# Attention scores: two heads side by side in two row halves of TensorE, in three products of 16-bit parts, in place of one head over all rows in two products of 32-bit parts

## The reference

```python
y = x * rsqrt(mean(x * x) + 1e-6) * rms_w
y = einsum('bsm,cm->bsc', y, w_in)                 # q: 32 heads, k: 8, v: 8, each of 64
q, k = rope(q), rope(k)
qk = einsum('bghsd,bgxpd->bghsp', q, k) * 64 ** -0.5
qk = where(causal, qk, -inf)
attn = softmax(qk, axis=-1)
o = einsum('bghsp,bgxpd->bghsd', attn, v)
y = einsum('bsc,mc->bsm', o, w_out)
x = layernorm(x + (x + y))
x = layernorm(x + einsum('bsd,od->bso', ternary(x), ternary(weight) + rram_variation))
```

## Time and profile before

| | |
|---|---|
| Time, median of 3 runs | 1427.19 us (1426.4 to 1428.69) |
| Span of the profiled execution, first to last instruction | 1425.4 us |
| PE busy | 1318.0 us, 92%, 7328 matmuls |
| DVE busy | 1147.2 us, 80% |
| ACT busy | 1116.3 us, 78% |
| POOL busy | 873.7 us, 61% |
| mean granted clock of TensorE | 0.982 of full speed |

### The profile page before, as it was taken

One profiled execution on the slowest core, in us unless ns is written; L12 is line 12 of the kernel. 1 busy time (PEld: TensorE's weight loads), 2 busy tenths in 40 slices (PEclk: granted clock), 3 DMA queues, 4 the chain that ended last, 5 costly groups with the idle time before them and its releaser, 6 DMA issues. The chain is left out here.

```text
span 1425.4 us, 25329 instructions
## 1 busy us (share of the span) xinstructions
PE 1318.0 (92%) x7328; PEld 838.4 (59%) x7328; DVE 1147.2 (80%) x3062; ACT 1116.3 (78%) x2327; POOL 873.7 (61%) x905
## 2 busy tenths in 40 slices
PE   4689999999999999999999999999999999898886
PEld 2456565665656565665656565666656566565554
DVE  4578887878887888878887888878788787887976
ACT  4768878788888888788887878788887888787664
POOL 1266667386645766386646766387646767786565
PEclk9799999999999999999999999999999999999998
DMA  6101111011101211021101211021100211210002
GB/s 199 27 20 38 64 30 31 27 57 45 37 21 45 59 29 31 23 60 44 36 24 26 72 35 31 23 60 43 38 24 23 75 35 37 61 42 27 18 33 85
DMA packets 45163, 61.82 MB, mean 43 GB/s; under 512 B 10464, under 2 KB 27104, under 8 KB 45024
## 3 DMA queue, kind: packets, MB, share of 16 engines
q1 hardware_dynamic: 45024, 60.20, 14.3%
HBM read 34.74 MB, written 4.46 MB: 27 GB/s over the span
## 5 line engine op out<-in xcount | busy, mean ns | idle before, releaser
L1100 DVE SCALAR_TENSOR_TENSOR prob_lo<-t,prob_hi 128x512 f16<-128x512 f32 x576 | 394.7, 686 | 76.0 <-ACT prob_hi L797 72.2
L797 ACT ACTIVATE prob_hi<-t 128x512 f16<-128x512 f32 x576 | 340.2, 591 | 146.1 <-PE t L1221 140.8
L1165 PE MATMUL s<-k_t,q_t 128*128 128x512 f32 (+3 forms) x1536 | 428.2, 383 | 23.8 <-DVE neg_max L1009 8.5
L829 ACT ACTIVATE prob<-prob,neg_max 128x896 f32<-128x896 f32 (+7 forms) x512 | 392.0, 767 | 7.2 <-DVE neg_max L1009 4.3
L1221 PE MATMUL t<-ident,prob 128*128 128x128 f32 x2304 | 350.8, 275 | 6.9 <-ACT prob L829 6.8
L1221 PEld LDWEIGHTS t<-ident,prob 128*128 128x128 f32 x2304 | 290.6, 143 | 109.7 <-ACT prob L829 13.2
L1009 DVE CUSTOM_DVE_ANT_0 prob<-s,mask 128x512 f32<-128x512 f32 (+3 forms) x512 | 289.6, 583 | 53.4 <-PE s L1165 33.3
L1165 PEld LDWEIGHTS s<-k_t,q_t 128*128 128x128 f32 x1536 | 244.9, 193 | 66.4 <-DVE neg_max L1009 19.0
L1136 PE MATMUL ot<-prob_lo,v_sb 128*128 128x512 f16 x576 | 221.0, 384 | 27.1 <-DVE prob_lo L1100 27.0
L1134 PE MATMUL ot<-prob_hi,v_sb 128*128 128x512 f16 x576 | 223.9, 389 | 0.9 <-DVE o_raw L1081 0.9
L770 POOL TENSOR_TENSOR o_lo<-o_raw,o_hi 128x256 f16<-128x256 f32 x128 | 86.2, 674 | 198.7 <-ACT o_hi L907 196.9
(11 more groups left out here) (106 smaller groups left out, 1841.4 us busy)
## 6 DMA issues: line engine op xcount, KB each, us to landing
swapped<-flat SPq DMA_DIRECT2D x320, 64.0 KB, 2.0
spread<-recip_rows SPq DMA_DIRECT2D x128, 128.0 KB
recip_rows<-turned SPq DMA_DIRECT2D x512, 0.5 KB
raw<-L_attn_w_in SPq DMA_DIRECT2D x8, 768.0 KB, 4.2
raw<-L_attn_w_out SPq DMA_DIRECT2D x8, 512.0 KB, 3.6
out<-acc SPq DMA_DIRECT2D x16, 256.0 KB, 2.0
acc<-L_attn_x SPq DMA_DIRECT2D x3, 1024.0 KB, 10.4
acc<-L_attn_x SPq DMA_DIRECT2D x4, 256.0 KB, 4.2
```

Of the source, the lines that this page charges most:

```text
L797: act.activation(prob_hi[:, u % 2, :], t_ps[u % 2][:, :], ACT.Copy, scale=P_SCALE).then_inc(prob_hi_done, 1)
L829: act.activation(row, row, ACT.Exp, bias=neg_max[:, kk % 4, h:h + 1], scale=-1.0, accum_out=total[:, kk % 4, h:h + 1]).then_inc(ex_done, 1)
L1100: dve.scalar_tensor_tensor(out=prob_lo[:, u % 2, :], in0=t_ps[u % 2][:, :], scalar=P_SCALE, in1=prob_hi[:, u % 2, :], op0=ALU.mult, op1=AL ...
L1165: mm = pe.matmul(s_ps[:, off:off + cols], q_t[:, h, s * P:(s + 1) * P], k_t[:, part, keys:keys + cols], start=(part == 0), stop=(part == 1))
```

## The change

The queries and keys are held in 16-bit floats (`F16`). `q_t` gets a new layout: in place of one block for each head with high and low part stacked on the rows, there is one block for each pair of heads and part: rows 0 to 63 are the even head, rows 64 to 127 the odd head. A score step is made for both heads of a pair at once, at the even head's place in the list; at the odd head's place TensorE does nothing. It is six matmuls of 64 rows: high x high, low x high, high x low, each for rows 0 to 63 into the first bank of `s_ps` and rows 64 to 127 into the second. Before them it waits until all steps before the pair have been read (`n` in place of `n - 1`). VectorE reads as before, each head at its own place, but its scale is a column (`neg_kappa`) and no constant, since `flat` now has a fixed scale that suits 16-bit floats. The high parts of the queries are one ScalarE copy of 128 rows, the low parts one subtraction of 128 rows; keys still take two each. `flat_scale` goes, `w_back` and `neg_kappa` take its place, once in a pass. The tables of places are not touched.

```diff
-MASKED = -1e30
+MASKED = -3e38
-V_SCALE = 2.0 ** -12
+Q_SCALE = 2.0 ** 10
+FLAT_SCALE = Q_SCALE / (Y_SCALE * W_SCALE)
...
-        q_t = sb("q_t", [P, HG, NT * P], F32R)
-        k_t = sb("k_t", [P, 2, 12 * P], F32R)
+        q_t = sb("q_t", [P, 2, HG // 2, NT * P], F16)
+        k_t = sb("k_t", [P, 2, 12 * P], F16)
...
-                                pool.tensor_tensor(q_t[DH:P, 2 * c, at], x[0:DH, :], q_t[0:DH, 2 * c, at].bitcast(F32),
-                                                   ALU.subtract).then_inc(part_lo, 1)
-                                wait(pool, part_lo, g, CHUNKS, n + 1)
-                                pool.tensor_tensor(q_t[0:DH, 2 * c + 1, at], x[DH:P, :],
-                                                   q_t[DH:P, 2 * c + 1, at].bitcast(F32), ALU.subtract
+                                pool.tensor_tensor(q_t[:, 1, c, at], x[:, :], q_t[:, 0, c, at], ALU.subtract
                                                    ).then_inc(parts_done, 1)
...
-                            wait(act, flat_scale_done, g, 1, 1 + b // 2)
-                            act.activation(flat[:, n % 2, :], bank[:, :], ACT.Copy,
-                                           scale=flat_scale[:, group, kind:kind + 1]).then_inc(flat_done, 1)
+                            act.activation(flat[:, n % 2, :], bank[:, :], ACT.Copy, scale=FLAT_SCALE
+                                           ).then_inc(flat_done, 1)
...
-                                act.activation(q_t[0:DH, 2 * c, at], x[0:DH, :], ACT.Copy)
-                                act.activation(q_t[DH:P, 2 * c + 1, at], x[DH:P, :], ACT.Copy).then_inc(parts_hi, 1)
+                                act.activation(q_t[:, 0, c, at], x[:, :], ACT.Copy).then_inc(parts_hi, 1)
...
+                            group = (g + b // 2) % 2
+                            wait(dve, kappa_done, g, 1, b // 2 + 1)
...
-                                                     scale=-DH ** -0.5, scalar=low_max[:, h:h + 1] if c else 3e38,
+                                                     scale=neg_kappa[:, group:group + 1],
+                                                     scalar=low_max[:, h:h + 1] if c else 3e38,
...
-                                dve.reciprocal(flat_scale[0:DH, n, 1:2], wy_scale[0:DH, :])
-                                dve.reciprocal(flat_scale[:, n, 0:1], wy_scale[:, :]).then_inc(flat_scale_done, 1)
+                                dve.reciprocal(w_back[:, n:n + 1], wy_scale[:, :]).then_inc(w_back_done, 1)
+                                wait(dve, w_back_done, g, 1, 2)
+                                dve.tensor_scalar(neg_kappa[:, n:n + 1], w_back[:, n:n + 1], w_back[:, n:n + 1],
+                                                  -DH ** -0.5 * (Y_SCALE * W_SCALE / Q_SCALE) ** 2, ALU.mult, ALU.mult
+                                                  ).then_inc(kappa_done, 1)
...
                             _, b, s, h, c = e
+                            if h % 2:
+                                continue
                             n = scored(b, s, h, c)
-                            cols, off = min(BANK, (s + 1) * P - c * BANK), n % 2 * BANK
+                            cols = min(BANK, (s + 1) * P - c * BANK)
...
-                            wait(pe, max_done, g, STEPS_MADE, n - 1)
-                            for part in range(2):
-                                mm = pe.matmul(s_ps[:, off:off + cols], q_t[:, h, s * P:(s + 1) * P],
-                                               k_t[:, part, keys:keys + cols], start=(part == 0), stop=(part == 1))
-                            mm.then_inc(sc_full, 1)
+                            wait(pe, max_done, g, STEPS_MADE, n)
+                            for turn, (q_part, k_part) in enumerate(((0, 0), (1, 0), (0, 1))):
+                                for a in range(2):
+                                    rows = slice(a * DH, (a + 1) * DH)
+                                    mm = pe.matmul(s_ps[:, a * BANK:a * BANK + cols],
+                                                   q_t[rows, q_part, h // 2, s * P:(s + 1) * P],
+                                                   k_t[rows, k_part, keys:keys + cols], start=(turn == 0), stop=(turn == 2))
+                                    if turn == 2:
+                                        mm.then_inc(sc_full, 1)
```

More of the change, by code:

```diff
@@ L326, in seq_block @@
         rms_s = sb("rms_s", [P, 2, KC])
-        flat_scale = sb("flat_scale", [P, 2, 2])
+        w_back = sb("w_back", [P, 2])
+        neg_kappa = sb("neg_kappa", [P, 2])
         out_scale = sb("out_scale", [P, 2])
@@ L369, in seq_block @@
         scales_done = sem("scales_done")
-        flat_scale_done = sem("flat_scale_done")
+        w_back_done = sem("w_back_done")
+        kappa_done = sem("kappa_done")
         o_scale_done = sem("o_scale_done")
@@ L616, in _ @@
             pool.memset(sums[:, 1, 1:2], 1.0).then_inc(ones_set, 1)
-            pool.memset(flat_scale[:, :, 1], V_SCALE).then_inc(ones_set, 1)
             pool.memset(recip[:, :, :], 0.0).then_inc(consts_set, 1)
@@ L751, in one @@
                                 at = k_half(b, half)
-                                pool.tensor_tensor(k_t[0:DH, 1, at], x[0:DH, :], k_t[0:DH, 0, at].bitcast(F32),
+                                pool.tensor_tensor(k_t[0:DH, 1, at], x[0:DH, :], k_t[0:DH, 0, at],
                                                    ALU.subtract).then_inc(part_lo, 1)
-                                wait(pool, part_lo, g, CHUNKS, n + 1)
-                                pool.tensor_tensor(k_t[DH:P, 1, at], x[0:DH, :], k_t[0:DH, 0, at].bitcast(F32),
+                                wait(pool, part_lo, g, 4, 2 * b + half + 1)
+                                pool.tensor_tensor(k_t[DH:P, 1, at], x[0:DH, :], k_t[0:DH, 0, at],
                                                    ALU.subtract).then_inc(parts_done, 1)
@@ L872, in one @@
                                 wait(act, v_hi_done, g, 4, 2 * b + half + 1)
-                            group, kind = (g + b // 2) % 2, c // 2
-                            wait(act, flat_scale_done, g, 1, 1 + b // 2)
-                            act.activation(flat[:, n % 2, :], bank[:, :], ACT.Copy,
-                                           scale=flat_scale[:, group, kind:kind + 1]).then_inc(flat_done, 1)
+                            act.activation(flat[:, n % 2, :], bank[:, :], ACT.Copy, scale=FLAT_SCALE
+                                           ).then_inc(flat_done, 1)
                         elif e[0] == "hl":
@@ L972, in events @@
                             if c < 2:
[L973 to L976, removed]
+                                dve.tensor_tensor(q_t[:, 1, c, at], x[:, :], q_t[:, 0, c, at], ALU.subtract
                                                   ).then_inc(parts_done, 1)
@@ L979, in events @@
                                 at = k_half(b, half)
-                                dve.tensor_tensor(k_t[0:DH, 1, at], x[0:DH, :], k_t[0:DH, 0, at].bitcast(F32),
+                                dve.tensor_tensor(k_t[0:DH, 1, at], x[0:DH, :], k_t[0:DH, 0, at],
                                                   ALU.subtract).then_inc(part_lo, 1)
-                                dve.tensor_tensor(k_t[DH:P, 1, at], x[0:DH, :], k_t[0:DH, 0, at].bitcast(F32),
+                                dve.tensor_tensor(k_t[DH:P, 1, at], x[0:DH, :], k_t[0:DH, 0, at],
                                                   ALU.subtract).then_inc(parts_done, 1)
@@ L1032, in events @@
                                 wait(dve, scales_done, g, 2, 4)
-                                if plan is first:
-                                    dve.wait_ge(ones_set, 3)
-                                dve.reciprocal(flat_scale[0:DH, n, 1:2], wy_scale[0:DH, :])
-                                dve.reciprocal(flat_scale[:, n, 0:1], wy_scale[:, :]).then_inc(flat_scale_done, 1)
+                                dve.reciprocal(w_back[:, n:n + 1], wy_scale[:, :]).then_inc(w_back_done, 1)
[3 more added lines that the diff above has]
+                                                  ).then_inc(kappa_done, 1)
                         elif e[0] == "wo":
@@ L1045, in events @@
                                 wait(dve, o_back_done, g, 1, 1)
-                                wait(dve, flat_scale_done, g, 1, 1)
-                                dve.tensor_scalar(out_scale[:, g % 2:g % 2 + 1], flat_scale[:, g % 2, 0:1], o_back[:, :],
-                                                  0.5 / V_SCALE, ALU.mult, ALU.mult).then_inc(out_scale_done, 1)
+                                wait(dve, w_back_done, g, 1, 1)
+                                dve.tensor_scalar(out_scale[:, g % 2:g % 2 + 1], w_back[:, g % 2:g % 2 + 1], o_back[:, :],
+                                                  0.5 / FLAT_SCALE, ALU.mult, ALU.mult).then_inc(out_scale_done, 1)
                         elif e[0] == "nw":
@@ L1183, in events @@
```

(2 more changed lines are left out.)

## The result

The changed kernel takes 1576.44 us (median of 4, 1574.87 to 1589.06) beside 1427.09 us for the kernel before: 149 us more. The ratio over all runs is 1.107, 95% interval 1.103 to 1.111; the quotient of the two medians is 1.105. The forecast was 1472 with a range from 1360 to 1560. The direction came true and the size did not. Rival B's sum, 1574, is nearly the measured time, but what it blamed is not what the runs show.

What follows compares the result with a forecast made beforehand. TensorE was taken to bound the kernel, with VectorE close behind. The terms -97 + 65 + 70 + 15 - 8 = +45 us, on the span of 1425.4 plus 1.8, gave 1472 us, range 1360 to 1560.

Steps and rivals of the forecast that it cites:

- Rival B: Each switch to row halves and back empties the array and bares the weight load: +167 us, 1574 us in all; chance 0.12.
- What bounds the kernel: TensorE, busy 92% of the span, is on the path, VectorE close behind; two score banks in turn are enough.
- Work of the score matmuls: TensorE's score products fall from 289 to 192 us with the row halves side by side: -97 us.
- Rival C: The row halves run one after the other, so score products cost +95 in place of -97: 1664 us; chance 0.05.
- Changing over: TensorE going to row halves and back at each pair: one array emptying of 0.17 us for each of 384 pairs, +65 us.
- The second bank: TensorE waits for all of VectorE's reads before a pair: between 0 and 174 us, taken at two fifths, +70 us.
- VectorE's column: VectorE's score read takes its scale from a column, 0.06 us more for 512 first-chunk steps, 31 us, half counted: +15 us.
- Splits: ScalarE saves one query copy of 627 ns for each of 64 chunks, GpSimd one subtraction: -8 us.

Runs made afterwards that it cites:

- e1: Kernel before, with only the even head of a pair waiting until all earlier score steps have been read: 1568.73 us, ratio 1.100.
- e2: e1 with the odd head's products moved to the even head's place, still over 128 rows in 32-bit parts: 1601.53 us, ratio 1.123.
- e7: Changed kernel with a pair's six 64-row products replaced by three over all 128 rows, leaving out half of each head's products: 1522.49 us.
- e8: Changed kernel with the edits of e5 and e7 at once: 1421.00 us, ratio 0.995 to the kernel before.
- e5: Changed kernel with VectorE reading both heads of a pair one right after the other at the even head's place: 1476.63 us, ratio 1.035.
- e4: Changed kernel with each head's three 64-row products at its own place and the banks in turn again: 1509.49 us, ratio 1.058.
- e6: Kernel before with its stacked layout, banks in turn and constant scale kept, only 16-bit parts and a power-of-two scale new: 1404.16 us, ratio 0.984.
- e3: Changed kernel with a constant, only near the right scale, in place of the scale column in VectorE's read: 1568.13 us, ratio 1.099.
- e9: e6 with the wait of e1, the even head waiting for all reads before it: 1531.49 us.

## Why the prediction was right in direction and wrong in size

The runs make a ledger from the kernel before to the changed one: the bank wait alone +142 (e1 against before), the pair at one place +33 (e2 against e1), the lighter products with 16-bit parts, fewer splits, the column and an earlier first bank -79 (e7 against e2), changing over with the later first bank +54 (changed kernel against e7). The sum is +150 against 149 measured. Each step starts where the last one ended, so that it closes is no proof. The first two steps differ in one thing each, the last two in several. What e8 shows is that the edits of e5 and e7 don't take out the same time twice.

*What bounds the kernel.* Right: TensorE was the full engine, and e4 and e6, in which nothing new waits, both move with its work. But from the small waits of the earlier trace rows I took it that two banks in turn are enough. They were only just enough: in 245 of 383 successions the turn was in use.

*Work of the score matmuls, -97.* Right in kind, and somewhat small: a pair of 512 costs three slots and two changeovers. The three slots of a pair of 128 columns take 0.17 us in e7, not the 0.33 that I gave them, which is 10 us over 64 pairs. An estimate from the starts in the traces, with idle time taken off, has 319 us of score products before and 207 in e7, so -112. In the time, the third ledger step gives -79 with the column in it, -87 without (8 us by e3), and the -8 that I gave the splits is inside that too. Rival C, halves one after the other, is out.

*Changing over, +65.* At most +54 in the time, with the first bank's delay in it. Each way costs TensorE 0.10 us, which is neither nothing nor the 0.17 that I took for an emptied array. The trace shows how: elsewhere a weight load starts ahead of its product, under the one before, by 0.214 us in the median where two products over all rows follow each other within 0.3 us. At the 360 ways into row halves and the 360 ways back (24 pairs stand directly behind another) it starts together with its product, 4 ns ahead in the median and at most 31.

```profile
684.34 0.10 PEld L1130 LDWEIGHTS ot<-prob_hi,v_sb 128*128 128x128 f16 x1 [0.42 <-issue]
684.34 0.39 PE L1130 MATMUL ot<-prob_hi,v_sb 128*128 128x512 f16 x1
...
685.11 0.10 PEld L1130 LDWEIGHTS ot<-prob_hi,v_sb 128*128 128x128 f16 x1
...
685.22 0.38 PE L1130 MATMUL ot<-prob_hi,v_sb 128*128 128x512 f16 x1
```

The first of these follows scores, the second a turning. The gap on each side of a pair is 0.10 us. A weight load of 16 bits is as long, 0.095 to 0.099, so whether the gap is an emptying or the load laid bare is not shown. Rival B was right about the loads: at none of the 720 changeovers did one run ahead by more than 31 ns. Its sum, which came near the measured time, did so by luck: it wanted 0.44 us for a pair and the trace has 0.19.

*The second bank, +70.* This is the step that failed: "I take two fifths". I had the raw figure, 174 us over 245 of 383 successions, and the trace after has 171 us more idle time ahead of scores. The wait alone costs 142 us in e1, four fifths of the raw figure; with the pair at one place it is 142 + 33 = 175. My reasons for discounting it were that VectorE is idle 20% of the span and would catch up. It can't, for the reason that I wrote next to it and did not follow: VectorE is not behind, it is in order. Its second read stands behind a low part, that behind ScalarE, that behind TensorE's turning, and TensorE is the one that waits. e5 shows it by moving only the reads: 100 us come back, with VectorE's work all but unchanged (1186 us busy for 1192). I had also said that VectorE's wait for scores would change little; it doubled, from 57.3 us to 118.6, which fits a round in which the engine that makes the scores is the one that waits for banks. What I didn't see at all is the 33 us of putting the odd head's products forward. I had even counted it as a gain, since the scores lie ready earlier.

*VectorE's column, +15.* The instruction grew as the earlier trace rows said, 683 to 746 ns without `low_max`, and from 746 to 805 with it, so that all 768 steps paid and not 512. The time paid 8 to 12 us. I overstated the share on the path.

*Splits, -8.* ACT's busy time fell by 51 us (1116 to 1065). No run has this alone; its price stays open.

*Left open.* TensorE's mean granted clock was 0.969 in the changed kernel and 0.982 before. It was 0.968 in e2 and e7 and 0.971 in e3, and 0.98 in e1, e4, e5, e8 and e9, while e1 is nearly as slow as the changed kernel; so in these runs the lower clock goes with the pair at one place and late reads. If all of e2's span of 1600.5 us went with the mean clock, 1600.5 x (1 - 0.968 / 0.980) = 20 of its 33 us would be the clock's, an estimate from these means that also counts the time in which other engines set the pace. What it was, and what the order was, no run separates.

## What to carry to other kernels

Before giving two buffers to one operation that had them in turn, measure in the trace how often the next fill starts ahead of the last read's end, and take that sum at nearly full price where the reader stands in a fixed order behind work that depends on the waiting engine: here it was 142 of 174 us, and the reader's idle time was no discount. If both results come at once, read them at once: move the reader's second read beside the first, which gave back 100 us. An experiment that takes out one cost should be looked through for what else it moves, as the first bank in e7. And look whether part of the change (here the 16-bit type, without the row halves) gives a gain with no new wait.

## What the runs showed of the hardware

Two 64-row products in different row halves and different banks ran fully side by side: a pair's six products took the same 0.75 us, changeover out included, as one head's three (the changed kernel, e4). They needn't be issued in turns for it: in e4 a head's three products started 10 ns after the first of the three that were issued ahead of them in the other half. Going from work over 128 rows to row halves and back took 0.10 us each, and the weight load that follows a changeover started at most 31 ns ahead of its product (360 each way), where elsewhere the median was 214. A column operand added 60 ns to VectorE's read of 512 columns (683 to 746), and a second column as much again (746 to 805). The copy of 128 rows and the copy of 64 rows took ScalarE the same time, 623 against 627 ns for 512 columns. In 32-bit parts the weight load of a score product took 193 ns and in 16-bit parts 95 to 99.
